# Row sums of four rounds at a time in a two-stage attention and expert kernel

## The reference

```python
attn = jnp.einsum('bhqd,bhkd->bhqk', q, k) / math.sqrt(HEAD_DIM)
attn = attn + alibi_bias(seq_len, N_HEADS)[None] + causal_mask(seq_len)[None, None]
attn = jax.nn.softmax(attn, axis=-1)
y = jnp.einsum('bhqk,bhkd->bhqd', attn, v)
...
idx = jnp.argmax(probs, axis=-1)          # one expert per token
x = x + _L0_attn_ref(xn, L0_attn_W_qkv, L0_attn_W_o) + _L0_ffn_ref(xn, L0_ffn_wg, L0_ffn_W, L0_ffn_b)
```

## Time and profile before

| | us |
|---|---|
| median of three runs (lowest, highest) | 1824.9 (1824.75, 1836.62) |
| profiled execution | 1827.11 |
| its span | 1825.4 |
| TensorE busy in it | 1687.3 (92%) |
| GpSimd busy in it | 675.6 (37%) |
| one group, repeating from the second on | 141.3 |

### The profile page before, as it was taken

How to read it: one execution, slowest core, us unless ns; L and a number is a source line. 1 busy time by engine, 2 the same in 40 slices (tenths; PEclk the granted TensorE clock), 3 DMA queues, 4 the chain that set the end, 5 groups by cost and what they waited for, 6 DMA issues and landing times. The chain is left out here.

```text
span 1825.4 us, 27949 instructions
## 1 busy us (share of the span) xinstructions
PE 1687.3 (92%) x9970; PEld 1015.6 (56%) x9971; DVE 1104.7 (61%) x2484; ACT 785.2 (43%) x1575; POOL 675.6 (37%) x643
## 2 busy tenths in 40 slices
PE   5999999579899999999999999999999999689898
PEld 4777777444444444454545444444554443568686
DVE  5333333468677767776876876876777710634466
ACT  2222222024354555564655555565556555411111
POOL 4500000006572552553444454355256256132360
PEclk9999999769999999999999999999999999899899
DMA  6655554744604503602701800900900500355596
GB/s 219 210 185 179 197 189 160 159 77 84 106 8 92 98 13 73 117 7 60 136 7 39 156 8 20 175 8 8 180 16 7 197 7 6 133 161 166 176 393 231
DMA packets 96927, 203.59 MB, mean 112 GB/s; under 512 B 10908, under 2 KB 28348, under 8 KB 91164
## 3 DMA queue, kind: packets, MB, share of 16 engines
q1 hardware_dynamic: 87592, 178.56, 37.8%
q0 software_dynamic: 9216, 23.47, 4.1%
HBM read 122.46 MB, written 79.01 MB: 110 GB/s over the span
## 5 line engine op out<-in xcount | busy, mean ns | idle before, releaser
L1021 ACT ACTIVATE probs_sb<-score_ps 128x512 f32<-128x512 f32 (+3 forms) x1280 | 606.8, 546 | 503.2 <-PE score_ps L1085 196.0
L917 POOL TENSOR_TENSOR pair_sum<-probs_sb 128x512 f32<-128x512 f32 x384 | 480.2, 1283 | 598.7 <-ACT probs_sb L1021 493.1
L940 DVE TENSOR_REDUCE part_max<-max_ps 128x1 f32<-128x512 f32 x768 | 474.2, 680 | 250.4 <-PE max_ps L1050 247.8
L1050 PE MATMUL max_ps<-k_aug,q_aug 104*128 104x512 f32 (+3 forms) x1280 | 534.1, 427 | 54.1 <-DMA q_aug<-q_rows_d 22.8
L1082 PE MATMUL score_ps<-q_aug,k_aug 106*128 106x512 f32 (+3 forms) x1280 | 494.3, 393 | 18.7 <-DMA q_aug<-max_lo 9.8
L1082 PEld LDWEIGHTS score_ps<-q_aug,k_aug 106*128 106x128 f32 x1280 | 243.7, 191 | 183.1 <-issue 112.1
L1050 PEld LDWEIGHTS max_ps<-k_aug,q_aug 104*128 104x128 f32 x1280 | 251.1, 197 | 160.7 <-DVE part_max L940 82.1
L1126 PE MATMUL acc_ps<-probs_sb,v_sb 128*32 128x512 f32 (+3 forms) x2560 | 294.6, 539 | 0.0
L936 DVE CUSTOM_DVE_ANT_0 max_ps<-max_ps,mask_row 128x384 f32<-128x384 f32 (+3 forms) x512 | 238.9, 515 | 57.1 <-PE max_ps L1050 55.6
L972 DVE RECIPROCAL acc_sb<-acc_sb 128x128 f32<-128x128 f32 x128 | 119.7, 940 | 76.6 <-ACT acc_sb L1005 76.6
L1126 PEld LDWEIGHTS acc_ps<-probs_sb,v_sb 128*32 128x32 f32 x2560 | 73.2, 110 | 117.4 <-issue 97.4
(11 more groups left out here) (173 smaller groups left out, 1737.8 us busy)
## 6 DMA issues: line engine op xcount, KB each, us to landing
k_aug<-k_hi_d SPq DMA_DIRECT2D x14, 1024.0 KB
q_aug<-q_hi_d SPq DMA_DIRECT2D x14, 1024.0 KB
slot_y_d<-y_rows SPq DMA_DIRECT2D x39, 256.0 KB, 2.0
xn_d<-xn SPq DMA_DIRECT2D x8, 1024.0 KB, 5.5
q_hi_d<-st_hi SPq DMA_DIRECT2D x32, 256.0 KB, 3.4
q_lo_d<-st_lo SPq DMA_DIRECT2D x32, 256.0 KB, 3.7
k_hi_d<-st_hi SPq DMA_DIRECT2D x32, 256.0 KB, 2.5
k_lo_d<-st_lo SPq DMA_DIRECT2D x32, 256.0 KB, 2.8
```

Of the source, the lines that this page charges most:

```text
L917: nc.gpsimd.tensor_tensor(pair_sum[:, p % 2, hh], probs[:, s0, hh], probs[:, s1, hh], ALU.add).then_inc(pair_added, 1)
L940: nc.vector.tensor_reduce(part_max[:, hh * QT + i, kc:kc + 1], max_ps[:, bank, 0:w], AX.X, ALU.max).then_inc(max_taken, 1)
L1021: nc.scalar.activation(probs[:, r % P_SLOTS, hh, off:CH], score_ps[:, (r * HG + hh) % S_BANKS, off:CH], ACT.Exp).then_inc(exp_done, 1)
L1050: nc.tensor.matmul(max_ps[:, bank, 0:w], q_aug[0:ROW_MAX, half, hh, i * P:(i + 1) * P], k_aug[0:ROW_MAX, half, hh, kc * CH:kc * CH + w], s ...
```

## The change

The full rounds are now taken in fours: `QUAD_OF` numbers them, six quads in a group (rounds 4 to 7, 12 to 15, 16 to 19, 24 to 27, 28 to 31, 32 to 35). GpSimd adds the first two rounds, then the third and then the fourth to that sum, four adds each; one product with ones serves all four rounds. A slot of `probs` is free when the add that read it is done (`added_by`). `normalise` stands before quads instead of pairs. The token numbers are placed in three pieces of 12, 12 and 8 tiles, behind quads 0, 2 and 5 of the first group. The eight DMAs with the first rows of maxima (group 0, c0) are issued on ScalarE's queue, before its first exponential. The first row sum of a chunk, which starts the accumulator, is found by `FIRST_SUM`.

```diff
+QUAD_OF = {r: p // 2 for r, p in PAIR_OF.items()}
+QUAD_LAST = [rounds[-1] for rounds in QUAD_ROUNDS]
+def added_by(r):
+    t = QUAD_OF[r]
+    return HG * (3 * t + max(1, QUAD_ROUNDS[t].index(r)))
...
                 load(0, 0)
-                max_rows(0, 0, 0)
                 groups(sp, step)
...
+                pieces = {0: range(0, 12), 2: range(12, 24), 5: range(24, NT)}
...
-                    for p in range(NPAIR + 1):
-                        if p in Y_BEFORE_PAIR:
+                    for t in range(NQUAD + 1):
+                        if t in Y_BEFORE_QUAD:
...
-                        if first and 1 <= p <= NT // SCATTERS:
-                            place_tokens(p - 1)
-                        r1 = PAIR_LAST[p]
-                        s0, s1 = (r1 - 1) % P_SLOTS, r1 % P_SLOTS
-                        if not (first and p < 2):
-                            pool.wait_ge(pair_used, used + (p - 1))
+                        r0, r1, r2, r3 = QUAD_ROUNDS[t]
+                        if not (first and t < 2):
+                            pool.wait_ge(quad_used, used + (t - 1))
                         for hh in range(HG):
                             pool.wait_ge(exp_done, exps + (r1 * HG + hh + 1))
-                            nc.gpsimd.tensor_tensor(pair_sum[:, p % 2, hh], probs[:, s0, hh], probs[:, s1, hh],
-                                                    ALU.add).then_inc(pair_added, 1)
+                            nc.gpsimd.tensor_tensor(quad_sum[:, t % 2, hh], probs[:, r0 % P_SLOTS, hh], probs[:, r1 % P_SLOTS, hh],
+                                                    ALU.add).then_inc(added, 1)
+                        for r in (r2, r3):
+                            for hh in range(HG):
+                                pool.wait_ge(exp_done, exps + (r * HG + hh + 1))
+                                pool.wait_ge(added, adds + (added_by(r) - 2 * HG + hh + 1))
+                                nc.gpsimd.tensor_tensor(quad_sum[:, t % 2, hh], quad_sum[:, t % 2, hh],
+                                                        probs[:, r % P_SLOTS, hh], ALU.add).then_inc(added, 1)
+                        if first and t in pieces:
+                            place_tokens(pieces[t])
...
-                            if e in PAIR_OF:
-                                act.wait_ge(pair_added, adds + ((PAIR_OF[e] + 1 - back * NPAIR) * HG))
+                            if e in QUAD_OF:
+                                act.wait_ge(added, adds + (added_by(e) - back * ADDS))
...
                 maxima(PLAN_BEFORE[0], BANKS_BEFORE, 0)
+                act.wait_ge(max_lo_done, 1)
+                for row, part in ((ROW_MAX, max_hi), (ROW_MAX + 1, max_lo)):
+                    for hh in range(HG):
+                        act.dma_start(q_aug[row:row + 1, 0, hh, 0:CH].bitcast(F32),
+                                      part[hh * TPC:(hh + 1) * TPC, 0].bitcast(F32)).then_inc(max_rows_loaded[0], 16)
                 groups(act, step)
...
-                    if r - 2 in PAIR_LAST.values():
-                        pair_product(PAIR_OF[r - 2], ROUNDS[r - 2] == (cc, 1), adds)
+                    if r - 2 in QUAD_LAST:
+                        quad_product(QUAD_OF[r - 2], r == FIRST_SUM[cc], adds)
```

More of the change, by code:

```diff
@@ L62 @@
 NPAIR = len(PAIR_OF) // 2
-PAIR_LAST = {p: r for r, p in PAIR_OF.items()}
+QUAD_OF = {r: p // 2 for r, p in PAIR_OF.items()}
+NQUAD = NPAIR // 2
+QUAD_ROUNDS = [[r for r in range(NR) if QUAD_OF.get(r) == t] for t in range(NQUAD)]
+QUAD_LAST = [rounds[-1] for rounds in QUAD_ROUNDS]
+ADDS = NQUAD * 3 * HG
+def added_by(r):
+    t = QUAD_OF[r]
+    return HG * (3 * t + max(1, QUAD_ROUNDS[t].index(r)))
+FIRST_SUM = [min(r for r, (cc, _) in enumerate(ROUNDS) if cc == c and (r not in QUAD_OF or r - 2 in QUAD_LAST))
+             for c in range(QC)]
 LAST_ROUND = [max(r for r, (cc, _) in enumerate(ROUNDS) if cc == c) for c in range(QC)]
@@ L152 @@
              for c in range(QC) for k in range(QUARTERS)}
-Y_BEFORE_PAIR = {min([p for p in range(NPAIR) if PAIR_LAST[p] > (LAST_ROUND[c] + 3 + QUARTERS) % NR] or [NPAIR]):
+Y_BEFORE_QUAD = {min([t for t in range(NQUAD) if QUAD_LAST[t] > (LAST_ROUND[c] + 3 + QUARTERS) % NR] or [NQUAD]):
                  ((LAST_ROUND[c] + 3 + QUARTERS) // NR, c) for c in range(QC)}
@@ L749, in attend @@
         probs = sb("probs_sb", [P, P_SLOTS, HG, CH], F32)
-        pair_sum = sb("pair_sum", [P, 2, HG, CH], F32)
+        quad_sum = sb("quad_sum", [P, 2, HG, CH], F32)
         part_max = sb("part_max", [P, QT * HG, QC], F32)
@@ L770, in attend @@
             sem("max_blank"), sem("neg_done"), sem("max_turned"), sem("max_hi_done"), sem("max_lo_done"))
[L771 to L772 removed]
+        scored, exp_done, pv_done, added, quad_used = (
+            sem("scored"), sem("probs_ready"), sem("pv_done"), sem("quad_added"), sem("quad_used"))
         experts_loaded = sem("experts_loaded")
@@ L886, in _, with place_tokens @@
                 pool.wait_ge(token_made, 1)
-                def place_tokens(k):
-                    for t in range(k * SCATTERS, (k + 1) * SCATTERS):
+                pieces = {0: range(0, 12), 2: range(12, 24), 5: range(24, NT)}
+                def place_tokens(tiles):
+                    for t in tiles:
                         pool.indirect_dma_start(m.slot_token_d, bass.IndirectOffsetOnAxis(ap=m.slot_cell[:, t:t + 1], axis=0),
@@ L899, in step @@
                 def step(g, half, first, last):
-                    exps, used = base(pool, g, NSU), base(pool, g, NPAIR)
-                    for p in range(NPAIR + 1):
-                        if p in Y_BEFORE_PAIR:
-                            back, cc = Y_BEFORE_PAIR[p]
+                    exps, used, adds = base(pool, g, NSU), base(pool, g, NQUAD), base(pool, g, ADDS)
+                    for t in range(NQUAD + 1):
+                        if t in Y_BEFORE_QUAD:
+                            back, cc = Y_BEFORE_QUAD[t]
@@ L1008, in step @@
                     events, banks = plan_of(g, last)
-                    units, rounds, adds = base(act, g, NSU), base(act, g, NR), base(act, g, NPAIR * HG)
+                    units, rounds, adds = base(act, g, NSU), base(act, g, NR), base(act, g, ADDS)
                     for r, (cc, jb) in enumerate(ROUNDS):
@@ L1087, in score_unit, with quad_product @@
                     last.then_inc(scored, 1)
-                def pair_product(p, start, adds):
+                def quad_product(t, start, adds):
                     for hh in range(HG):
-                        pe.wait_ge(pair_added, adds + (p * HG + hh + 1))
-                        last = nc.tensor.matmul(den_ps[hh * DH:(hh + 1) * DH, :], m.ones[:], pair_sum[:, p % 2, hh],
+                        pe.wait_ge(added, adds + (added_by(QUAD_LAST[t]) - HG + hh + 1))
+                        last = nc.tensor.matmul(den_ps[hh * DH:(hh + 1) * DH, :], m.ones[:], quad_sum[:, t % 2, hh],
                                                 start=start, stop=False)
-                    last.then_inc(pair_used, 1)
+                    last.then_inc(quad_used, 1)
                 def probs_of(g, r, exps):
@@ L1104, in has_row_sums @@
                 def has_row_sums(r):
-                    return r not in PAIR_OF or r - 2 in PAIR_LAST.values()
+                    return r not in QUAD_OF or r - 2 in QUAD_LAST
                 def row_sums(g, r, exps, adds):
@@ L1111, in row_sums @@
                     probs_of(g, r, exps)
-                    if r - 2 in PAIR_LAST.values():
-                        pair_product(PAIR_OF[r - 2], ROUNDS[r - 2] == (cc, 1), adds)
-                    if r not in PAIR_OF:
+                    if r - 2 in QUAD_LAST:
+                        quad_product(QUAD_OF[r - 2], r == FIRST_SUM[cc], adds)
+                    if r not in QUAD_OF:
                         for hh in range(HG):
                             nc.tensor.matmul(den_ps[hh * DH:(hh + 1) * DH, off:CH], m.ones[:],
-                                             probs[:, r % P_SLOTS, hh, off:CH], start=jb == 0, stop=r == LAST_ROUND[cc])
+                                             probs[:, r % P_SLOTS, hh, off:CH], start=r == FIRST_SUM[cc], stop=r == LAST_ROUND[cc])
                 def value_products(g, half, r, exps):
@@ L1134, in step @@
                     pe.wait_ge(v_loaded[half], 16 * (g // 2 + 1))
-                    exps, adds = base(pe, g, NSU), base(pe, g, NPAIR * HG)
+                    exps, adds = base(pe, g, NSU), base(pe, g, ADDS)
                     taken = base(pe, g, NMU), None if last else base(pe, g + 1, NMU)
```

5 lines of the change are left out of this document (1 added, 4 removed).

## The result

The changed kernel takes 1815.3 us (median of seven runs, 1808.3 to 1816.5) beside 1829.9 us for the kernel before (seven runs of the same job). The ratio is 0.9917, with a 95% interval of 0.9893 to 0.9940. I had forecast 0.9% less; it is 0.8% less. The 1824.9 us that I started from is the median of the first three of those seven runs. The profiled execution took 1816.46 us, with a span of 1814.7 instead of 1825.4, so it gained 10.7 us where the medians gained 14.6.

The account below looks back on a forecast made before the run. TensorE's instruction list was taken as the path. Middle groups 17.2, start 9.7, less last group 4.2, group 0 5.0 and clock 1.7, gave 16.0 us: 1824.9 to 1808.9 us, own range 1801 to 1816, 8 in 10 within 1789 to 1826.

Parts of the forecast that it names:

- Products removed: Six of twelve products with ones per group leave TensorE, 0.86 us each: 5.2 us per group, 41 us in all.
- Adds and their stalls in the middle: GpSimd's longer adds give back 2.3 of 5.2 us per middle group; each gains 2.9 us, six of them 17.2.
- three late score tiles: Fourth score tiles of rounds 23, 35 and 39 in middle groups stall TensorE by 0.5, 1.2 and 0.6 us.
- rival of dearer chained adds: Adds waiting for GpSimd's own semaphore cost more each; from 0.09 us the gain is gone, 0.2 gives 1845.7; chance 0.10.
- the one in which the adds hide: Late exponentials don't reach TensorE: middle groups give 31 us, the last breaks even, time 1789 us; chance 0.17.
- The start: First rows of maxima issued on ScalarE's queue: the first score starts at 380.7 instead of 390.44, 9.7 us gained.
- The other end, no gain: At the start, the rows land when they land now, because the loads are not through: 9.7 us less gain.
- Token numbers: In group 0, twelve indirect DMAs ahead of c0's multiplication delay c2's rows and group 1's load: 5.0 us lost.
- The last group: Without work on maxima the chain of adds shows in full: round 39's fourth score tile later, 4.2 us lost.
- The clock: Stalls in the last group invite one stretch at half speed, 3.4 us long: 1.7 us lost.
- one in each of them as the other end: One low-clock stretch in each middle group too: 10 us more lost.

Follow-up runs that it names:

- e5: The change with the fourth round of each quad left out of the row sums, eight adds instead of twelve: 1798.36 us, ratio 0.9812 to the kernel before.
- e4: e3 with c1's multiplication moved behind quad 2 and c2's behind quad 5: 1789.48 us, ratio 0.9808 to the kernel before.
- e1: The kernel before, with only the first rows of maxima moved to ScalarE's queue, pairs kept: 1815.66 us, ratio 0.9951.
- e3: The change with the token numbers' twelve indirect DMAs behind c0's multiplication instead of ahead of it: 1802.56 us, ratio 0.9888 to the kernel before.
- e2: The change with the first rows of maxima back on SP's queue, so the quads alone: 1823.77 us, ratio 0.9990 to the kernel before.
- e10: The changed kernel unchanged, timed again in a third job on a third chip: 1814.2 us, ratio 0.9930 to the kernel before.
- e8: The kernel of e4 unchanged, timed again in the third job: 1791.1 us, ratio 0.9799 to the kernel before.
- e6: The change with pairs instead of quads in the last group only: 1822.12 us, ratio 0.9947 to the kernel before.
- e7: e4 with pairs instead of quads in the last group: 1805.37 us, ratio 0.9862 to the kernel before.
- e11: The kernel of e6 unchanged, timed again in the third job: 1809.1 us, ratio 0.9895 to the kernel before.
- e9: The kernel of e7 unchanged, timed again in the third job: 1785.4 us, ratio 0.9771 to the kernel before.

## Why the prediction was right, and where it was not

**Products removed.** 384 records fewer. With the chain of adds out of the way (e5, and e4 with all adds kept) a middle group repeats every 136.3 to 136.4 us, 4.9 to 5.0 less than before. Forecast 5.2: right.

**Adds and their stalls in the middle.** A quad takes 14.92 us, forecast 14.9. I had named the three late score tiles with 0.5, 1.2 and 0.6 us; their waits are 0.21, 0.94 and 0.65 in group 3, and the third is 0.35 to 0.38 in the others. Where the clock stayed up, the period is 138.2, forecast 138.4. e5 (shorter chains) and e4 (chains that start sooner) confirm the cause from two sides. The rival of dearer chained adds falls: adds that wait for GpSimd's own semaphore follow at 1.24 us like the others. So does the one in which the adds hide; it would have shown 136.

**The start.** Forecast 9.7, measured 10.0 at the first score and 9.0 us of the whole in e1. The other end, no gain, rested on the eight rows not passing the loads. They were issued by 372.5 and had landed by 379.5. The Trainium skill (DMA: Bandwidth & Descriptors, section "Issuing engines are not separate DMA queues") has a second issuer save only issuing time, usually little; here SP's list stood ahead, with one issue of 14.48 us in it (14.06 in the kernel before), and what was saved was the wait behind it. So the page's sentence fits what was saved and not that it is small; the other end, which I had read out of it, did not come.

**Token numbers.** c0's multiplication ends at 431.9, forecast 432. The wait for the load of group 1 is 5.74, forecast 6. The first score of c2 waits 4.5 us, where I forecast 7 to 8. TensorE was ready for it at 433.9, where my steps had 432.0 (up to there some 15 us ran at half speed, in the kernel before some 5), and the rows had landed by 438.4, where they had 439.8. Counted from the first score, the first unit of group 1 is 10.1 us later than before, forecast 9.7, and what lies behind it gives 3.7 back, forecast 4.7: a loss of 6.4, forecast 5.0. The mechanism is confirmed by e3: with the twelve DMAs behind the multiplication that unit comes 9 us sooner.

**The last group.** Forecast 4.2 for stalls and 1.7 for the clock, 5.9 together; measured 6.7. Up to c3's first add it is 0.6 us longer than before, where I had 0.7 less. From that add to round 39's fourth score tile it takes 46.1 us instead of 41.7, which is 4.4 more; my steps had 46.6 (1503.45 to 1550.0). From there to the last product it takes 7.1 instead of 5.4, 1.7 more, with the clock at 0.50 for 3.4 us from 1534.4 on. So the chain of adds sets c3's length, as forecast, and the clock costs what was forecast in this execution; in e2, e3 and e10 this end took 8.3 to 8.4 us, with 6.8 us at 0.50. Two of the five low-clock stretches lie inside the chain, where GpSimd adds without a pause, and cost nothing: the same chain took 46.1 us in those three too, with other stretches in it.

**The clock** in the middle groups is the term that was mis-sized. I gave the clock 1.7 us, one stretch in the last group, and none in the middle groups, with one in each of them as the other end. Read in stretches of 1 us, from the first score to the end of the last group, the record has some 63 us at half speed, before some 22 (the earlier trace rows are one of them). Half of the difference is 20 us, and an upper bound of what was lost, since much of it lies where TensorE waits anyway: in group 0 ahead of the unit that waits for its load, and in the last group inside c3's chain. Against the forecast the middle groups came out 4.9 us worse, group 0 1.4 and the last group 0.8; the start and what lies behind came out 1.8 better. The three low-clock stretches of the middle groups, 10.2 us at half speed, are 5.1 us and explain the first of these.

**The number.** The time is 6.4 us above the forecast, inside its own range of 1801 to 1816. That difference is mostly one of starting points: seven runs put the kernel before at 1829.9, three had put it at 1824.9. The medians gained 14.6 us of the forecast 16.0, the profiled execution 10.7. That the medians come so near is in part luck, since the trace, from which the terms were worked, shows 5 us less gained than their sum.

**Right for the reason given?** For the most part: start, stalls, token numbers and last group each show at their place. What the forecast did not say is how little of the change's main part was left. By e2 the quads by themselves are worth 0.1%, with an interval that includes no change at all; the change's gain is mostly that of the start, while what the quads saved in the middle groups (15 us in e2, 12 in the change) was given back in group 0 and the last group. My own sum had that in it (17.2 less 4.2, 5.0 and 1.7 leaves 6.3), but it put the quads first.

## What to carry to other kernels

When work moves from a full engine to an idle one, look for the place in the idle engine's list where something that others wait for stands behind it. Here reordering that list (token numbers behind c0's multiplication, the multiplications of c1 and c2 behind later quads) was worth 23 us (e8 beside e10), where the change itself brought 12 in that job, without one instruction fewer. Use the longer chain only where other work fills the wait: in the last group, which has none, pairs were better than quads (by 5 to 6 us of the whole, with intervals that overlap). And compare versions in one job on one chip: e6 and e7 looked like losses until they ran beside their parents.

## What the runs showed of the hardware

- Short waits and low clock lie together, but not always. In the last group of the change three waits of 1.4 to 1.8 us were each followed within 1.3 us by 3.4 us at a granted clock of 0.50. In e10 a wait of 1.64 us, up to 1475.80, was followed by a clock of 1.00 until 1515. With pairs the waits are at most 0.7 us, and there are fewer such stretches: none in e1, e7 and e11, one before and in e9, two in e6. So the waits are not their only cause.
- Low clock costs time only where TensorE sets the pace. In a middle group one stretch of 3.4 us at 0.50 made the group 1.6 to 1.9 us longer (140.1 beside 138.2 in the change, 140.1 beside 138.3 in e10, 142.9 beside 141.3 in e1). Inside c3's chain of adds in the last group it made no difference: 46.1 us in the change, e2, e3 and e10.
- In group 0 the same program was granted 0.91 and 0.94 (the change and e10), and its length was 207.0 and 203.2 us; for e4 and e8 it was 192.8 and 199.7. Differences of a few us in that group say little about an edit.
- Eight DMAs of 2 KB landed within 7 us of their last issue (372.5 to 379.5), while loads of 256 KB and 1 MB were under way. The load in front of the list had held them, not the transfers.
- ScalarE and VectorE can stand still together for 7 to 14 us without a release in the profile that ends it. The same programs (e7 and e6) had it on one chip and not on another (e9 and e11), in one traced execution each.
